# AdaLN two-layer network: the expert ranking of layer 0 in groups of four and two batches, its steps spread between the attention's row maxima

## What is computed

```python
h = _layernorm(x) * (1 + ca) + sa                      # per batch, adaLN
k = (h @ w_dk + b_dk) @ w_uk + b_uk                    # v alike; q = h
attn = softmax(rope(q) @ rope(k).T / sqrt(8))          # 16 heads of 8
x = x + ga * ((attn @ v) @ w_o + b_o)
h = _layernorm(x) * (1 + cb) + sb
logits = h @ gate_w                                    # [T, 8]
top_vals, top_idx = top_k(logits, 2)
# multiplier of each choice: softmax over the experts whose logit
# is within 2 * JITTER of the threshold, relative to max(|logit|, thr)
x = x + gb * sum over the 2 chosen experts of weight * expert(h)
```

## Time and profile before

| what | us |
|---|---|
| median of 3 runs | 3187.78 (3186.58 to 3188.36) |
| profiled execution, its own time | 3188.66 |
| its span | 3186.8 |
| attention stage, to the first load of the experts | 718.4 |
| engines busy over the span: TensorE, VectorE, ScalarE, GpSimd | 2736.1, 2522.3, 2245.9, 2264.0 |

### The profile page before, as it was taken

The page is one execution under the profiler, slowest core; times in us unless marked ns, Lnnn a source line. Parts: engine busy times, 40 slices in busy tenths (PEclk is TensorE's granted clock), DMA queues, the critical chain, the costliest instruction groups (busy, mean ns, idle before and its releaser), DMA issues. The chain is left out here.

```text
span 3186.8 us, 56520 instructions
## 1 busy us (share of the span) xinstructions
PE 2736.1 (86%) x18747; PEld 2087.0 (65%) x18747; DVE 2522.3 (79%) x3550; ACT 2245.9 (70%) x4091; POOL 2264.0 (71%) x1731
## 2 busy tenths in 40 slices
PE   5999999939999967898888989889888887779984
PEld 3555555518999834666666666666666666669983
DVE  5788888733444446999999999999999999968993
ACT  2677777612222249999998998989999998656652
POOL 3346667562333348999999999999999999733574
PEclk7999999959999989999999999999999999889996
DMA  5555555315666562222222222222222222222222
GB/s 140 108 106 112 116 112 114 83 52 192 193 192 198 165 213 83 78 78 71 84 80 82 81 71 83 79 83 81 74 79 81 81 84 78 90 62 82 69 75 56
DMA packets 209194, 322.00 MB, mean 101 GB/s; under 512 B 37787, under 2 KB 118071, under 8 KB 204283
## 3 DMA queue, kind: packets, MB, share of 16 engines
q1 hardware_dynamic: 195666, 299.13, 34.5%
q0 software_dynamic: 12224, 18.42, 2.0%
q10 hardware_dynamic: 1008, 0.72, 0.1%
HBM read 269.92 MB, written 55.84 MB: 102 GB/s over the span
## 5 line engine op out<-in xcount | busy, mean ns | idle before, releaser
L1779 POOL TENSOR_TENSOR resid_x<-s_ux,s_B_rows 128x1024 f32<-128x1024 f32 x256 | 605.7, 2366 | 87.5 <-PE s_y L2509 86.8
L2340 DVE TENSOR_TENSOR_SCAN resid_x<-s_dA,resid_x 128x1024 f32<-128x1024 f32 x256 | 581.6, 2272 | 29.3 <-ACT s_dA L1991 21.6
L2348 DVE TENSOR_TENSOR_SCAN resid_x<-s_late,s_back_in 128x1024 f32<-128x1024 f32 x256 | 583.4, 2279 | 22.2 <-ACT s_late L2001 16.8
L2509 PE MATMUL s_y<-identity,resid_x 128*128 128x128 f32 x4096 | 562.4, 283 | 10.1 <-issue 6.9
L2509 PEld LDWEIGHTS s_y<-identity,resid_x 128*128 128x128 f32 x4096 | 502.6, 147 | 65.8 <-issue 37.9
L1787 POOL TENSOR_TENSOR resid_x<-resid_x,s_C_rows 128x1024 f32<-128x1024 f32 x192 | 454.5, 2367 | 1.1 <-DVE resid_x L2340 1.1
L2355 DVE TENSOR_TENSOR resid_x<-resid_x,s_C 128x1024 f32<-128x1024 f32 x320 | 382.2, 1194 | 10.3 <-PE s_C L2484 6.5
L2496 PE MATMUL s_back_in<-identity,resid_x 128*128 128x128 f32 x2048 | 296.5, 292 | 99.2 <-ACT resid_x L2012 55.0
L775 DVE TENSOR_REDUCE a_row_max<-a_maxscores 128x2 f32<-128x512 f32 x512 | 335.0, 682 | 58.9 <-PE a_maxscores L971 55.4
L1991 ACT ACTIVATE s_dA<-s_dt,s_A 128x510 f32<-128x510 f32 x512 | 330.1, 676 | 71.8 <-DVE resid_x L2340 70.4
L2001 ACT ACTIVATE s_late<-s_dt,s_A 128x510 f32<-128x510 f32 x512 | 338.1, 710 | 0.0
(11 more groups left out here) (464 smaller groups left out, 5700.8 us busy)
## 6 DMA issues: line engine op xcount, KB each, us to landing
s_B_rows<-forward_rows SPq DMA_DIRECT2D x256, 256.0 KB, 3.3
e_w<-L_ffn_w_by_expert SPq DMA_DIRECT2D x71, 768.0 KB, 4.5
s_C_rows<-forward_rows SPq DMA_DIRECT2D x192, 256.0 KB, 3.4
a_Q<-split_qk SPq DMA_DIRECT2D x96, 192.0 KB
split_qk<-a_parts SPq DMA_DIRECT2D x32, 384.0 KB
e_x<-slot_inputs SPq DMA_DIRECT2D x71, 132.0 KB
a_K<-split_qk SPq DMA_DIRECT2D x64, 128.0 KB
s_late<-choice_outputs SPq DMA_DIRECT2D x16, 512.0 KB, 4.9
```

The source lines that it names most:

```text
L1779: tt(R[s, 0], ux[par][:], brow[s % BRING][:].unsqueeze(1).broadcast_to([P, C2, W]), ALU.mult).then_inc(S["in_ready"], 1)
L2340: nc.vector.tensor_tensor_scan(r, a, r, 0.0, ALU.mult, ALU.add).then_inc(S["scanned"], 1)
L2348: nc.vector.tensor_tensor_scan(r[:, ::-1], a[:, ::-1], b[:, ::-1], 0.0, ALU.mult, ALU.add).then_inc(S["scanned"], 1)
L2509: last = mm(YP[:, t, c2 * P:(c2 + 1) * P], R[s, d][:, c2, t * P:(t + 1) * P], core.ident[:], is_transpose=True, start=((s, d) == (0, 1) an ...
```

## The change

The groups become four batches wide in the first half (batches 0 to 15) and stay two wide in the second. The rows that wait for their scatter lie in one ring of tiles for 16 batches instead of a ring of four buffers of one group each. Variance, root and offset go on in pairs of batches, and a batch is normalized in the turn of its pair's root (from turn 8 on). The two choices are cut into three pieces of two steps each, and each piece stands behind another row maximum; a group of four has its first choice in one turn (12, 16, 20, 24), its second in the next (13, 17, 21, 25) and its ranking in the third (14, 18, 22, 26). A group of two has both choices in one turn (26, 28, 30, 32) and its ranking in the next (27, 29, 31, 33); the last four groups are chosen and ranked in the same turn (34, 35, 37, 39). The weights' steps move from behind row maximum 9 to behind row maximum 6. A single norm moves on ScalarE behind the copies of V, its modulation on GpSimd behind the rotary product. From turn 32 on all of a turn's scatters stand at its end.

```diff
 class FrontPlan:
-        self.groups = [(lo, lo + 2) for lo in range(0, B, 2)]
+        wide = B // 2
+        self.groups = [(lo, lo + 4) for lo in range(0, wide, 4)] + [(lo, lo + 2) for lo in range(wide, B, 2)]
...
-            rooted = self.groups[self.group_of[b]][1] + last
-            i = max(rooted if rooted > B else rooted + 1, self.norm_at[b - 1] if b else 0)
-            while held.get(i, 0) >= (2 if i >= B else 1):
+            rooted = b // 2 * 2 + 2 + last
+            i = max(rooted, self.norm_at[b - 1] if b else 0)
+            while held.get(i, 0) >= (2 if i > B else 1):
...
-        self.choose_at = {self.norm_at[hi - 1] + 1: g for g, (_, hi) in enumerate(self.groups)}
-        self.rank_at = {self.norm_at[hi - 1] + 2: g for g, (_, hi) in enumerate(self.groups)}
-        self.turns = self.norm_at[B - 1] + 4
+        for g, (lo, hi) in enumerate(self.groups):
+            i = self.norm_at[hi - 1]
+            self.first_at[i + 1] = g
+            self.second_at[i + 2 if hi - lo == 4 else i + 1] = g
+            if i > B:
+                self.quick_at[i + 1] = g
+            else:
+                self.rank_at[i + 3 if hi - lo == 4 else i + 2] = g
+        self.turns = self.norm_at[B - 1] + 3
         for i in range(self.turns):
-            ranked = sum(1 for turn in self.rank_at if turn < i)
+            ranked = sum(1 for turn in [*self.rank_at, *self.quick_at] if turn < i)
             open_rows = 2 * TC * self.groups[ranked - 1][1] if ranked else 0
             sent = min(open_rows, sent + (4 if i <= B else 6)) if i < B + last else open_rows
```

In a turn of GpSimd:

```diff
-                    if plan.late(i) is not None:
-                        modulate(plan.late(i))
-                    scatters(sent, (sent + due) // 2)
+                    half = (sent + due) // 2 if i < B else sent
+                    scatters(sent, half)
                     if live(i, 0):
...
                         nc.gpsimd.tensor_tensor(qcos[:], qk[:].rearrange("p a t -> p (a t)"), cos[:], ALU.mult).then_inc(S["cos_done"], 1)
+                    if plan.late(i) is not None:
+                        modulate(plan.late(i))
...
-                    scatters((sent + due) // 2, due)
+                    scatters(half, due)
```

In a turn of ScalarE:

```diff
                     exponentials(i, 0)
                     if i in plan.root_at:
                         root(plan.root_at[i])
+                    exponentials(i, 1)
                     if plan.early(i) is not None:
                         second_norm(plan.early(i))
-                    if plan.late(i) is not None:
-                        second_norm(plan.late(i))
-                    exponentials(i, 1)
...
                         last.then_inc(S["v_ready"], 1)
+                    if i in plan.rank_at:
+                        distances_raised(plan.rank_at[i])
+                    if plan.late(i) is not None:
+                        second_norm(plan.late(i))
                     exponentials(i, 3)
```

In a turn of VectorE:

```diff
                     row_max(i, 6)
+                    if i in plan.rank_at:
+                        weights(plan.rank_at[i])
                     row_max(i, 7)
...
-                    if i in plan.rank_at:
-                        weights(plan.rank_at[i])
+                    if i in plan.first_at:
+                        top_of(plan.first_at[i], 0)
                     row_max(i, 10)
-                    if i in plan.choose_at:
-                        first_choice(plan.choose_at[i])
+                    if i in plan.first_at:
+                        first_of_top(plan.first_at[i], 0)
...
                     row_max(i, 12)
+                    if i in plan.first_at:
+                        first_chosen(plan.first_at[i])
                     row_max(i, 13)
-                    if i in plan.choose_at:
-                        second_choice(plan.choose_at[i])
+                    if i in plan.second_at:
+                        top_of(plan.second_at[i], 1)
                     row_max(i, 14)
+                    if i in plan.second_at:
+                        first_of_top(plan.second_at[i], 1)
                     row_max(i, 15)
+                    if i in plan.second_at:
+                        second_chosen(plan.second_at[i])
+                    if i in plan.quick_at:
+                        places(plan.quick_at[i])
+                        distances(plan.quick_at[i])
+                        slot_rows(plan.quick_at[i])
+                        limits(plan.quick_at[i])
+                        weights(plan.quick_at[i])
```

At the end of a turn of TensorE:

```diff
                         last.then_inc(S["y_ps"], 1)
+                    if i in plan.quick_at:
+                        if plan.late(i) is not None:
+                            pe.wait_ge(S["f_hT"], plan.late(i) + 1)
+                        counts(i, plan.quick_at[i])
```

135 lines of the change are left out of this document (71 added, 64 removed).

## The result

The change made the kernel slower: 3226.45 us (median of 4; 3225.80 to 3231.88) against 3188.07 us for the kernel before (median of 4; 3186.58 to 3208.05), a ratio of 1.0096 with a 95% interval of [1.0062, 1.0130]. Forecast were 3187.4 us and a range to 3197. The profiled execution took 3231.88 us, its span 3230.0 us, against 3188.66 and 3186.8.

What follows compares the result with a forecast made beforehand. In the attention stage's pipelined middle TensorE is 94% busy, VectorE 86%. Terms -10.3 + 0.4 - 0.2 + 4.1 + 5.1 + 0.5 = -0.4 us gave a median of 3187.4 us; range 3177 to 3197.

Steps and rivals of the forecast that it cites:

- the ranking turns of four: Turns 14, 18, 22: 18.0 us each, the weights held until 8.6 us into the turn, TensorE's wait about the old one.
- the third rival: Eight ranking turns: limits' last step starts after GpSimd's product, held 1.2 us, row max 7 late; +10, 3198 us; chance 0.17.
- the 2.26 us: GpSimd's wait for VectorE, which the moved norm and modulation were said to fill at no cost.
- turns with both choices: Turns 28 and 30, both choices of two batches: 18.6 us each, like a first choice, the rest behind row max 13.
- the first choice: Turns 12, 16, 20, 24, four batches: 18.7 us each, comparison held 0.4, last steps held inside GpSimd's third part.
- the second choice: Turns 13, 17, 21, 25, four batches: all steps behind row max 13, 17.0 us each, between 16.9 and 17.7.
- rankings of two: Turns 27, 29, 31, which rank two batches: 17.8 us each.
- The first rival: First-choice steps slip in ahead of GpSimd: 7 turns lose 1.2 us less, -8.4, 3179.0 us; chance 0.24.
- The norm in the root's turn: Logits begin in turn 9 instead of 10: +0.4 us; norm and modulation themselves cost nothing.
- The tail: From turn 33 to the experts' first load: -0.2 for turn 33, +4.1 ranking at once, +5.1 scatters, +0.5 variance.
- The four scatters: End of the stage: 26 scatters in a row behind the last norm turns instead of 22, 4 x 1.28 = +5.1 us.
- The term for the ranking at once: Turns 34, 35, 37, 39: ranking ahead of the next bias sum makes turn 36 4.1 us late, passed to GpSimd's chain.

Runs made afterwards that it cites:

- f0: The changed kernel run again without an edit, a third time, on another set's chip; 1.0079 of the kernel before.
- f1: The changed kernel with all four scatters of the turn ahead of a ranking put ahead of the rotary product; 1.0040 of the kernel before.
- e1b: The changed kernel with the limits ahead of row max 5 and the weights back behind row max 9; 1.0066 of the kernel before.
- e3: The changed kernel with the last groups ranked a turn after their choice, not at once; 1.0066 of the kernel before.
- g2: The changed kernel with groups of two batches throughout, last groups still ranked at once, a repeat; 0.9958 of the kernel before.
- g6: The changed kernel with groups of two throughout and last groups ranked a turn after the choice, a repeat; 0.9949 of the kernel before.
- e4: The changed kernel with limits and weights moved, and in turn 32 the last batch's loads issued ahead of the row-maxima stores; 1.0055 of the kernel before.
- e6: The changed kernel with groups of two throughout and last groups ranked a turn after the choice, first run; 0.9938 of the kernel before.
- h3: The changed kernel with groups of two throughout and last groups ranked a turn after the choice, third run; 0.9965 of the kernel before.
- h1: The changed kernel with limits and weights moved and up to 12 scatters a turn instead of 6 from turn 33 on; 1.0048 of the kernel before.

## Why the prediction was wrong

**The step that failed** is the cost of the ranking turns of four, "18.0", with its sentence that the weights "are held until 8.6 us into the turn". I had the limits' last step ahead of the product, as in the earlier trace rows (446.03 and 446.50), and put its being late into the third rival at 1.2 us of hold in eight turns. Three things were missing. The step was held in the three turns of four batches that have scatters around them (even turns, gate at 3.3 us), not in the ranking turns of two (odd turns, gate at 0.5). It was held through two GpSimd operations: 2.35 us, and 2.4 us of the turn. And I had no term at all for TensorE's clock: two falls, of 5.3 and 3.5 us in the turn of the wait (18; 26 against f0's, where the step was held and the clock stayed) and of 8.0 and 5.7 in the next, added 22.5 us to the 7 of the three holds. Without the clock the three turns would have been 1.7 us each above the forecast's 18.0, 18.0 and 19.5: the larger part of the miss is the clock. f1 and e1b take away the hold from its two sides, and both restore turns 18 and 22 to 17.1 to 17.7 us.

The cause of the lateness stood in the trace of before and I did not use it: GpSimd's two scatters behind the variance, which delay the gate of the next turn. I wrote that norm and modulation fill the 2.26 us in which GpSimd waited; that gap is a plain turn's, ahead of the rotary sum. Where scatters stand around a ranking, the product came right behind one of them already (446.50 in the earlier trace rows, no idle time). The gate of that turn 24 in the kernel before:

```profile
439.77 0.98 POOL L576 DMA_INDIRECT slot_inputs<-a_choice_rows,a_slots  x1 [0.30 <-issue]
440.76 0.76 POOL L592 TENSOR_TENSOR a_y<-a_y,a_gate_rows 128x256 f32<-128x256 f32 x1
```

The turn began at 438.71, so this gate was 2.0 us into it.

**The third rival** had the step and GpSimd's two operations. It expected a step that comes after the product's start; the step came 0.22 us before it and was held longer than that. It counted eight turns where there were three, and its price was too low: 3198 where the kernel took 3226.

**The other terms of turns 11 to 32** held. Plain turns took 16.86 (16.85 forecast); turns with both choices 18.67 (18.6); the first choice 18.83, and 19.15 or 19.16 in turns 16, 20 and 24 (18.7), since the comparison for the maximum was held 1.00 us where I had 0.4; the second choice 17.51 (17.0), since the candidates behind row max 14 were held for 0.48; rankings of two 17.1 (17.8). These cancel: e1b, whose turn 26 took 20.40 (19.5) and turn 32 15.16 (16.5), has 390.0 against 390.8, so that the sum is close is in part luck. The first rival, steps that slip in ahead of GpSimd, is refuted for the last step of a first choice of four, which took 1.18 us (turns 12, 16, 20, 24). In turns 28 and 30 it came true: the step began 0.05 us ahead of the third part and took 0.19. These turns still took 18.67 and 18.68, so the forecast's 18.6 for them is right for another reason than the one it gives.

**The norm in the root's turn** cost the 0.4 us in turn 9 (16.86 against 16.41), and turn 10 of the first profile has another 0.4, which stays unexplained (e1b has none).

**The tail** was forecast at +9.5 us with its parts and came to +14.6. The four scatters are there as counted (26, 33.0 us from the first start to the last, against 27.9 for 22), and the variance's wait too (16.7 against 16.0 us from turn 37's bias sum to the last modulation). Not foreseen were 1.3 us between the last scatter and the experts' load (8.47 against 7.16), and 7.7 us in turns 33 to 36, where I had 3.9 (4.1 - 0.2); 2.5 of them are turn 33, whose scatters now stand in a row (below). The term for the ranking at once, 4.1, counted only what it delays; e3 beside the first profile and g2 beside g6 show a balance of about zero.

**Where the expected gain went:** with groups of two the middle gives 8 to 13 us, and ranked a turn later the tail is as before (109.4 to 117.5 us against 110.0 and 116.1). The groups of four add nothing in the middle even with limits and weights moved (390.0 in e1b against 388 to 393), open rows later, leave 26 scatters for the end, and put the ranking into the turns in which GpSimd's chain has no gap.

**What stays open.** Why the clock fell behind some of these waits and held behind others of the same length, in the same kernel and turn, no row here shows. Nor does one show what stopped VectorE at the end of turn 33, where row maxima 14 and 15 and the bias sum began 1.0, 2.5 and 3.6 us behind the products they need (by those products' recorded ends):

```profile
641.30 0.69 DVE L798 TENSOR_REDUCE a_row_max<-a_maxscores 128x2 f32<-128x512 f32 x1 [1.20 <-issue]
643.49 0.69 DVE L798 TENSOR_REDUCE a_row_max<-a_maxscores 128x2 f32<-128x512 f32 x1 [1.50 <-remote]
646.36 0.43 DVE L921 TENSOR_TENSOR a_y<-a_proj,a_bias_out 128x256 f32<-128x256 f32 x1 [2.17 <-remote]
```

The last two waits are in f0, e3, e4 and f1 within 0.1 us. No run was aimed at them, but the runs say what they go with, GpSimd's scatters in a row beside a full clock. In these five profiles six scatters stand in a row there, and turn 33 took 19.4 to 19.6 us. The kernel before has them three and three, no such wait, and 17.0 us. Groups of two (g2, e6, g6, h3) have four in a row, the wait ahead of row max 15 (1.42 to 1.53 us), none ahead of the bias sum, and 17.3 or 17.4 us. h1 has twelve in a row, and 2.21 us ahead of row max 15 and this ahead of the bias sum:

```profile
620.64 0.42 DVE L921 TENSOR_TENSOR a_y<-a_proj,a_bias_out 128x256 f32<-128x256 f32 x1 [4.27 <-remote]
```

So that all of a turn's scatters stand at its end from turn 32 on, which the prediction priced at nothing, is the likely cause of turn 33's 2.5 us. It is not shown: no run splits them again with all else left as it is.

## What to carry to other kernels

A step that is moved into a gap must be checked against the other engine's queue in the turns where that queue is fullest: the gap of a plain turn was gone in the turns that mattered, and GpSimd operations back to back can hold a VectorE step for two of them (2.35 us in the turns where the limits were held, 1.64 to 1.68 where the mask was). Price a wait of the bounding engine with what can follow from it too, here a turn or two at half clock, which cost several times the wait. Where a row of transfers is issued from one engine's queue, look at what the others do beside it. And before widening groups, count what opens later and lands in the tail.
